# Cross-attention and FP4 FFN on one Trainium2 core: the hidden layer h quantized whole, one step behind its tile, and each engine's step written in a new order

## The chip, the cores and the metric

The kernel runs on one NeuronCore of one Trainium2 chip. The metric is the time on the device in microseconds (us), the median of several executions. The engines named below are TensorE (PE, matmuls), VectorE (DVE), ScalarE (ACT), GpSimd (POOL) and SyncE (SP, which here issues nearly all DMAs).

## What is computed

```python
x = x + attention(layernorm(x), ctx, mask)      # 16 heads of 32, 77 keys per batch
x = x + ffn(layernorm(x))                       # x is (4, 2048, 512)

def ffn(x):
    gate = fp4_linear(x, w_gate)                # 512 -> 1408
    y = fp4_linear(x, w_up)                     # 512 -> 1408
    h = silu(gate) * y
    return fp4_linear(h, w_down)                # 1408 -> 512

def fp4_linear(x, w):                           # both operands quantized in blocks of 16
    return fp4_quant_dequant(x) @ fp4_quant_dequant(w).T

def fp4_quant_dequant(x):                       # per block of 16 along the last axis
    scale = max(max(abs(block)) / 6, 1e-12)
    return round_to_grid(block / scale) * scale # grid 0, .5, 1, 1.5, 2, 3, 4, 6, with sign
```

The attention applies its projections Wq, Wk, Wv and Wo with biases, a softmax over the unmasked keys, and masks by batch 0's key lengths.

## The kernel before

**Tiles.** The 8192 rows of x are 64 tiles of 128 rows (16 tiles a batch). Every matmul operand is split into two bf16 halves, HI and LO, and a product is three matmuls (HI·HI, HI·LO, LO·HI; `split_product`, L537). The weights are quantized and transposed once, in the first 200 us; the last rows of the gate and up weights are woven into the first three steps (`weave`).

**A software pipeline.** One `step` works on six tiles at once, each in a different stage. In step s they are m = s+3 (first layernorm), n = s+2 (q, scores, softmax), a = s+1 (probabilities times v, output projection, residual, second layernorm, quantizing x), f = s (gate and up), d = s-1 (down projection) and e = s-2 (output). The same step is written out once for every engine; each engine runs its own list in order, and semaphores connect the lists. So a wait that is not met holds everything that stands behind it on that engine.

**TensorE (L604 to L689)** does in a step: probabilities times v of tile a (pv, 144 small matmuls), q of n, gate/up chunk 0 of f, mask and scores of n, output projection of a, gate/up chunk 1, the first 15 matmuls of the down projection of d (`down_part(0)`), gate/up chunks 2 and 3, and the last 18 matmuls of the down projection (`down_part(1)`). A gate/up chunk is 352 of the 1408 columns, 24 matmuls. Chunks 0, 1 and 3 share the PSUM banks 0 and 1; chunk 2 uses banks 2 and 3, which belong to the scores and to pv too. So chunk c+1 and the next pv wait until VectorE has read the earlier chunk (`h_done`).

**VectorE (L1091 to L1132)** multiplies silu(gate) by up (`h_chunk`, L1048), and quantizes h in two parts: columns 0 to 639 (part A) at the end of the step of tile f, once two chunks are there; columns 640 to 1407 (part B) in the following step. A part takes top (absolute maxima of the blocks, L875), scale (L881), inverse (L891), divide (L895), two rounding passes (L901, L905), rescale (L909) and the LO half (`half_low`, L863). Between divide and the first rounding ScalarE squares (L702); between rescale and the LO half ScalarE writes the HI half (L829, L853). The quantization of the 512 columns of x for tile a has the same chain.

**ScalarE** also applies silu (L771), the exponentials (L777), the HI halves of the probabilities (L784), and the application of both norms (L811, L832). Silu and exponential use different tables, so each step has two table loads. **GpSimd** computes the reciprocal root of both norms in three small instructions (L505, L507, L509) and adds the output bias to the residual's copy of x (L520).

**SyncE (L355 to L420)** issues one DMA after another and waits for each one's input in turn. The HI and LO halves reach TensorE through a transposing DMA (`transposed`, L353): of the attention output (oT), the normed x (xnT), the probabilities (pT, in two pairs), both parts of h (hT) and the quantized x (xqT). In the first step of a batch SyncE also issues the 12 loads of that batch's v (`load_values`, L306), right behind oT. hT has one buffer for each part, written again only after the down matmuls have read it.

**Probabilities.** The 77 keys are laid in 3 blocks of 32 (KJ = 3, KW = 96), so that a row group of 32 partitions holds one block; ScalarE and VectorE write all 96 columns of 8 heads, 768 elements a pair.

## Time and profile before

| what | before |
|---|---|
| median of 3 runs | 2188.06 us (2186.34 to 2188.51) |
| the profiled execution | 2190.24 us, its span 2188.5 us |
| PE busy | 1954.9 us, 89% of the span |
| DVE busy | 1884.1 us, 86% |
| ACT busy | 1191.9 us, 54% |
| POOL busy | 395.2 us, 18% |
| mean share of the DMA engines in use, 1200 to 1800 us | 54% |
| mean granted TensorE clock | 0.961 of 2.4 GHz |

The span runs from the first instruction to the last. Busy shares are means over three different stretches: the preparation of the weights (up to about 200 us, with PE at 12 to 20 us in 50), 59 steps of nearly equal length, and four shorter steps at the end in which the pipeline empties. The granted clock of TensorE is 1.00 in the steps and between 0.53 and 0.69 from 50 to 200 us. Among the page's groups of instructions, the matmuls of the down projection stand out on TensorE: 84.5 us of idle time right before them, 80.6 of which ended with a transposing DMA of h.

### The profile page before, as it was taken

The numbers are of one execution on the slowest core, as the hardware profiler recorded it, in microseconds if no ns is written. First come the engines' busy times: TensorE is split into PE (matmuls) and PEld (weight loads), VectorE is DVE, ScalarE is ACT, GpSimd is POOL, SyncE is SP. The second block draws the span as 40 slices with busy tenths as digits, with TensorE's granted clock in tenths as the row PEclk, the third lists the DMA queues.
The fourth block names the chain that finished last, engine by engine and source line by source line (L and its number), as shares of the span: only waits on it lengthen the run. The fifth ranks groups of instructions, "written<-read, shape, count | busy, mean of one in ns | idle before, by whom it ended". The sixth has DMA issues, their size and how long they took to land.

```text
span 2188.5 us, 63466 instructions
## 1 busy us (share of the span) xinstructions
PE 1954.9 (89%) x24768; PEld 1228.0 (56%) x24960; DVE 1884.1 (86%) x3188; ACT 1191.9 (54%) x2617; POOL 395.2 (18%) x523
## 2 busy tenths in 40 slices
PE   6334899999998999999998999999999999999987
PEld 4222556666565656665565566665655566665654
DVE  7767889898987898988987898989888898988975
ACT  4534556655664566555664566556654566556631
POOL 4543111111111111111111111111111111111100
PEclk9656999999999999999999999999999999999999
DMA  5322665555555555555545555555545555555543
GB/s 168 80 68 64 106 125 126 115 114 115 124 113 107 122 124 118 118 108 127 121 98 122 121 127 115 113 115 124 123 102 122 122 127 117 111 118 121 121 90 63
DMA packets 663013, 248.19 MB, mean 113 GB/s; under 512 B 614870, under 2 KB 615894, under 8 KB 662974
## 3 DMA queue, kind: packets, MB, share of 16 engines
q1 hardware_dynamic: 661390, 247.67, 51.3%
q8 instruction: 24, 0.39, 0.1%
q10 hardware_dynamic: 1584, 0.01, 0.0%
q14 instruction: 15, 0.12, 0.0%
HBM read 65.97 MB, written 34.82 MB: 46 GB/s over the span
## 4 chain that ended last, share of the span: by engine, by line
DVE 23%; PE 19%; issue 18%; DMA 12%; ACT 12%; POOL 9%; SPq 7%; another core or an unknown queue 1%; ACTq 0%; POOLq 0%; DVEq 0%
PE psum L539 13%; DMA ph_room<-h_room 11%; SPq L353 5%; DVE h_room L895 4%; PE psum L630 4%; DVE neg_max L1054 4%; ACT L771 3%; DVE p_h L863 3%; POOL ln_rstd L507 3%; ACT silu_g L771 2%; POOL ln_var_eps L505 2%; ACT io_room L811 2%; ACT p_h L784 2%; POOL h_room L480 2%; DVE ln_stats L1018 2%
## 5 line engine op out<-in xcount | busy, mean ns | idle before, releaser
L610 PE MATMUL psum<-wguT,t_room 128*128 128x352 bf16 x6144 | 947.9, 313 | 4.5 <-DVE h_room L1048 1.1
L610 PEld LDWEIGHTS psum<-wguT,t_room 128*128 128x128 bf16 x6144 | 598.3, 98 | 327.8 <-DVE h_room L1048 2.0
L539 PE MATMUL psum<-wdT,ph_room 128*128 128x512 bf16 x1985 | 469.3, 385 | 84.5 <-DMA ph_room<-h_room 80.6
L539 PEld LDWEIGHTS psum<-wdT,ph_room 128*128 128x128 bf16 x2112 | 203.8, 99 | 336.5 <-DMA ph_room<-h_room 103.4
L505 POOL TENSOR_TENSOR ln_var_eps<-ln_mean_var,eps 128x1 f32<-128x1 f32 x128 | 64.5, 504 | 1618.7 <-DVE ln_mean_var L1020 1077.0
L702 ACT ACTIVATE h_sq<-h_room 128x640 bf16<-128x640 f32 (+3 forms) x158 | 121.1, 767 | 247.1 <-DVE h_room L895 247.1
L777 ACT ACTIVATE probs<-psum,neg_max 128x77 f32<-128x77 f32 x1024 | 235.0, 350 | 11.2 <-DVE neg_max L1054 10.4
L539 PE MATMUL psum<-t_room,wqT 128*128 128x128 bf16 x3072 | 188.3, 222 | 2.3 <-issue 1.0
L771 ACT ACTIVATE silu_g<-psum 128x352 f32<-128x352 f32 x256 | 117.3, 458 | 119.9 <-PE psum L610 119.2
L539 PEld LDWEIGHTS psum<-t_room,wqT 128*128 128x128 bf16 x3072 | 178.2, 100 | 7.2 <-issue 1.4
L539 PE MATMUL psum<-woT,t_room 128*128 128x512 bf16 x704 | 165.8, 385 | 14.5 <-issue 9.7
L895 DVE SCALAR_TENSOR_TENSOR h_room<-h_room,h_sc 128x640 f32<-128x640 f32 (+1 forms) x128 | 150.9, 1179 | 4.4
L1048 DVE TENSOR_TENSOR h_room<-silu_g,psum 128x352 f32<-128x352 f32 x256 | 132.1, 516 | 17.1 <-ACT silu_g L771 9.5
L797 ACT CAST halves<-q_room 128x512 bf16<-128x512 f32 x64 | 39.6, 618 | 185.1 <-DVE q_room L1035 185.1
L863 DVE TENSOR_TENSOR h_room<-h_room 128x640 bf16<-128x640 f32 (+1 forms) x128 | 113.7, 889 | 28.0 <-ACT h_room L853 27.0
L853 ACT CAST h_room<-h_room 128x640 bf16<-128x640 f32 x64 | 46.4, 725 | 154.2 <-DVE h_room L909 154.2
L863 DVE TENSOR_TENSOR p_h<-probs,p_h 128x768 bf16<-128x768 f32 x128 | 123.6, 965 | 5.1 <-ACT p_h L784 2.2
L539 PEld LDWEIGHTS psum<-woT,t_room 128*128 128x128 bf16 x768 | 70.8, 99 | 86.6 <-issue 4.7
L905 DVE SCALAR_TENSOR_TENSOR h_room<-h_sq,h_room 128x640 f32<-128x640 bf16 (+1 forms) x128 | 113.5, 887 | 2.2
L909 DVE TENSOR_TENSOR h_room<-h_room,h_sc 128x640 f32<-128x640 f32 (+1 forms) x128 | 112.1, 876 | 2.3
L901 DVE SCALAR_TENSOR_TENSOR h_room<-h_sq,h_room 128x640 f32<-128x640 bf16 (+1 forms) x128 | 112.8, 881 | 1.0 <-ACT h_sq L702 0.9
L875 DVE TENSOR_REDUCE h_sc<-h_room 128x40 f32<-128x640 f32 (+1 forms) x128 | 112.8, 881 | 0.0
(100 smaller groups left out, 2471.5 us busy)
## 6 DMA issues: line engine op xcount, KB each, us to landing
io_room<-in_x_dram SPq DMA_DIRECT2D x128, 256.0 KB, 2.7
x_scratch<-x_new SPq DMA_DIRECT2D x64, 256.0 KB, 2.0
x_cur<-x_scratch SPq DMA_DIRECT2D x64, 256.0 KB, 3.4
out_dram<-io_room SPq DMA_DIRECT2D x64, 256.0 KB, 2.7
t_room<-halves SPq DMA_TRANSPOSE x192, 3.1
raw<-in_L_ffn_w_down_dram SPq DMA_DIRECT2D x4, 704.0 KB, 4.4
raw<-in_L_ffn_w_gate_dram SPq DMA_DIRECT2D x11, 256.0 KB, 2.7
raw<-in_L_ffn_w_up_dram SPq DMA_DIRECT2D x11, 256.0 KB, 3.0
```

What stands on the lines that cost most here:

```text
L539: ins = pe.matmul(dst, left(i), right(j), start=first and n == 0, stop=last and n == len(PRODUCTS) - 1)
L610: ins = pe.matmul(ps[:, 0:CW], xqT[:, i, kc, :], wguT[:, which, j, kc, cols], start=(kc == 0 and i == j), stop=(kc == KC - 1 and i == LO))
L702: act.activation(dst, val, ACT.Square, scale=GRID_SLOPE).then_inc(done, 1)
L771: act.activation(silu_g[:, c % 2, :], gate_ps[c][:, 0:CW], ACT.Silu).then_inc(silu_done, 1)
L777: ins = act.activation(probs[:, h, 0:KEYS], score_ps[:, r, g, :], ACT.Exp, bias=neg_max[:, h:h + 1])
L863: return own.did(dve.tensor_tensor(dst, ps, high, ALU.subtract), signal, value)
L875: step_of(job, dve.tensor_reduce(job.sc[:, 0, 0:job.nb], blocks(job.src), AX_X, ALU.max, apply_absolute_value=True))
L895: step_of(job, dve.scalar_tensor_tensor(blocks(job.val), blocks(job.src), TIES_DOWN, spread(job.sc, 2, job.nb), ALU.mult, ALU.mult), job.d ...
L901: step_of(job, dve.scalar_tensor_tensor(job.tot, job.sq, GRID_BASE, job.val, ALU.add, ALU.subtract))
L905: step_of(job, dve.scalar_tensor_tensor(job.tot, job.sq, GRID_BASE, job.tot, ALU.add, ALU.subtract))
L909: step_of(job, dve.tensor_tensor(blocks(job.res), blocks(job.tot), spread(job.sc, 1, job.nb), ALU.mult), job.done)
L1048: own.did(dve.tensor_tensor(h[:, c * CW:(c + 1) * CW], silu_g[:, c % 2, :], up_ps[c][:, 0:CW], ALU.mult), h_done, f * CHUNKS + (c + 1))
```

## The change

- h is quantized whole (1408 columns) in the step behind its tile, where it was two parts in two steps. The semaphores of the two parts become one set; each of the eight kinds of instruction runs once, on 1408 columns and 88 blocks; the two transposing DMAs of h become one.
- The down projection runs one step later: for tile e = s-2 instead of d, all 33 matmuls in one piece, behind the output projection and ahead of gate/up chunk 1. Chunks 1, 2 and 3 then follow one another. `tile_out` stays with tile e, and moves to a later place in the step.
- The 77 keys are laid in 3 blocks of 26 (KN = 26) inside the row groups of 32. ScalarE and VectorE write 3·26·8 = 624 elements a pair in place of 768; the columns that are left out are set to zero once at the start by GpSimd. Number and shape of the matmuls of pv stay.
- DVE, ACT and SP run their step in a new order; the two norms' statistics get other work between their two instructions. GpSimd's add to the residual copy (L520) now waits for the HI half of q as well (`qT_hi`).
- The weights' quantization uses a scale tile of its own (`w_sc`), with the same instructions.

The core of the diff:

```diff
@@ SyncE, step @@
+                def probabilities(pair):
...
                 weave("norm")
                 if a is not None:
                     after(o_lo, a + 1)
...
                 if values is not None:
                     after(pv_done, GH * n)
                     load_values(values)
+                if e is not None:
+                    after(out_ready, e)
+                    after(x1_stored, 16 * e + 16)
+                    sp.dma_start(x1_cur[:], one(x1_scratch, e)).then_inc(x1_loaded, 16)
+                weave("scores")
+                weave("first")
+                if keys is not None:
+                    after(s_ps, GH * n + GH)
+                    load_keys(keys)
+                if n is not None:
+                    probabilities(0)
                 if m is not None and existing(m + 1) is not None:
                     after(xn_ready, m + 1)
                     sp.dma_start(x_in, one(x_t, m + 1)).then_inc(x_loaded, 16)
+                if n is not None and existing(n + 1) is not None:
+                    after(mask_ready, n + 1)
...
+                    sp.dma_start(mask_raw[:], one(mask_t, j + 1 if keys is None else 0)).then_inc(mask_loaded, 16)
+                if n is not None:
...
+                    probabilities(1)
+                if m is not None:
+                    after(xn_lo, m + 1)
+                    after(q_ps, m)
+                    transposed(xnT.rearrange("p s k t -> p (s k) t"), xn_h.rearrange("p s d -> p (s d)"), xnT_loaded)
+                weave("end")
                 if e is not None:
                     after(out_ready, e + 1)
                     sp.dma_start(one(out_t, e), out_sb).then_inc(out_stored, 16)
                 if a is not None:
                     after(x1_done, a + 1)
                     sp.dma_start(one(x1_scratch, a), x1_new[:]).then_inc(x1_stored, 16)
                     if existing(a + 1) is not None:
                         sp.dma_start(xb, one(x_t, a + 1)).then_inc(xr_loaded, 16)
...
                     after(xq_lo, a + 1)
                     after(gu_ps, a * CHUNKS)
                     transposed(xqT.rearrange("p s k t -> p (s k) t"), xq_h.rearrange("p s d -> p (s d)"), xqT_loaded)
...
+                if d is not None:
+                    after(h_lo, d + 1)
+                    after(down_done, d)
+                    transposed(hT.rearrange("p s k t -> p (s k) t"), h_h.rearrange("p s w -> p (s w)"), hT_loaded)
@@ GpSimd, step @@
                     pool.wait_ge(xr_loaded, 16 * a + 16)
+                    if n is not None:
+                        pool.wait_ge(qT_hi, n + 1)
                     own.did(pool.tensor_tensor(xb, xb, bo_all[:], ALU.add), xb_ready, a + 1)
@@ TensorE, step, behind the output projection @@
+                weave("first")
+                if e is not None:
+                    pe.wait_ge(hT_loaded, 16 * e + 16)
+                    at_least(pe, out_ready, e)
+                    for k in range(IC):
+                        ins = split_product(down_ps, lambda s: hT[:, s, k, :], lambda s: wdT[:, s, k, :],
+                                            k == 0, k == IC - 1)
+                    ins.then_inc(down_done, 1)
                 if f is not None:
                     pe.wait_ge(h_done, f * CHUNKS + 1)
                     gate_up_chunk(1)
-                if d is not None:
-                    pe.wait_ge(hA_loaded, 16 * d + 16)
-                    at_least(pe, out_ready, d)
-                    down_part(0).then_inc(downA_done, 1)
-                weave("first")
-                if f is not None:
                     if n is not None:
                         pe.wait_ge(exp_done, 2 * n + 1)
                     gate_up_chunk(2)
                     pe.wait_ge(h_done, f * CHUNKS + 2)
                     gate_up_chunk(3)
-                if d is not None:
-                    pe.wait_ge(hB_loaded, 16 * d + 16)
-                    down_part(1).then_inc(down_done, 1)
@@ VectorE, step @@
                 run(a, normalised)
                 run(m, first_norm)
+                run(a, half_low, o_h, o_sb, o_hi, o_lo, a)
+                run(d, top, hj, (h_done, d * CHUNKS + CHUNKS) if d is not None else None)
+                run(m, first_norm_end)
                 weave("norm")
...
                 run(n, q_low)
+                run(d, scale, hj)
+                run(d, inverse, hj)
                 run(n, maximum, 0)
+                run(d, divide, hj)
                 run(n, maximum, 1)
                 weave("scores")
...
                 run(a, residual)
                 run(a, second_norm)
+                run(f, h_chunk, 0)
+                run(a, second_norm_end)
+                weave("first")
+                run(d, first_round, hj)
+                run(d, second_round, hj)
+                run(d, rescale, hj)
+                run(a, top, xj, (xn2_ready, a + 1) if a is not None else None)
+                run(a, scale, xj)
+                run(a, inverse, xj)
+                run(n, probabilities_low, 0)
                 run(m, half_low, xn_h, xn, xn_hi, xn_lo, m)
...
                 run(a, divide, xj)
+                run(n, probabilities_low, 1)
+                run(e, tile_out)
                 run(f, h_chunk, 1)
...
                 run(a, first_round, xj)
                 run(a, second_round, xj)
                 run(a, rescale, xj)
                 weave("end")
...
+                run(d, half_low, h_h, hq, h_hi, h_lo, d)
                 run(f, h_chunk, 2)
                 run(a, half_low, xq_h, xq, xq_hi, xq_lo, a)
...
                 run(f, h_chunk, 3)
```

The order of ScalarE's step after the change, tiles in brackets: HI half of the attention output (a); mask (n); q HI (n); silu 0 (f); exponentials of half 0 (n); square of h (d); first 4 exponentials of half 1; first norm and HI half of x (m); second norm `xn2` (a); HI half of probabilities pair 0; last 4 exponentials; HI half of h (d); HI half of pair 1; silu 1 (f); square of x (a); silu 2; HI half of the quantized x (a); silu 3.

## Rows read from the trace of the kernel before

**Rows 1.** VectorE groups, 1200-1800 us: instruction, count, busy us, mean ns, idle before.

```profile
L1048 DVE TENSOR_TENSOR h_room<-silu_g,psum 128x352 f32<-128x352 f32 x78 | 40.3, 516 | 2.6
L863 DVE TENSOR_TENSOR p_h<-probs,p_h 128x768 bf16<-128x768 f32 x40 | 38.2, 955 | 0.9
...
L895 DVE SCALAR_TENSOR_TENSOR h_room<-h_room,h_sc 128x768 f32<-128x768 f32 x20 | 31.4, 1572 | 0.7
L1054 DVE TENSOR_REDUCE neg_max<-psum 128x8 f32<-128x616 f32 x40 | 30.0, 793 | 0.0
...
L895 DVE SCALAR_TENSOR_TENSOR h_room<-h_room,h_sc 128x640 f32<-128x640 f32 x19 | 15.7, 825 | 0.7
...
L1068 DVE TENSOR_TENSOR x_new<-psum,io_room 128x512 f32<-128x512 f32 x20 | 13.7, 684 | 0.0
```

**Rows 2.** ScalarE groups, same view, same stretch.

```profile
L777 ACT ACTIVATE probs<-psum,neg_max 128x77 f32<-128x77 f32 x320 | 73.5, 351 | 0.2
...
L771 ACT ACTIVATE silu_g<-psum 128x352 f32<-128x352 f32 x78 | 35.8, 458 | 32.2 <-PE psum L610 32.0
L784 ACT CAST p_h<-probs 128x768 bf16<-128x768 f32 x40 | 33.1, 828 | 0.6
...
L777 ACT ACT_TABLE_LOAD x20 | 25.7, 1283 | 0.4
...
L829 ACT CAST h_room<-h_room 128x768 bf16<-128x768 f32 x20 | 16.9, 847 | 0.0
```

**Rows 3.** TensorE's down matmuls, same view, same stretch.

```profile
L539 PE MATMUL psum<-wdT,ph_room 128*128 128x512 bf16 x603 | 141.3, 382 | 22.5 <-DMA ph_room<-h_room 21.3 <-issue 0.2
```

**Rows 4.** TensorE timeline, one step: start us, length us, instructions, idle before.

```profile
1500.91 1.32 PE L630 MATMUL psum<-v_cur,ph_room 32*128 32x33 bf16 x144
...
1509.90 2.54 PE L539 MATMUL psum<-woT,t_room 128*128 128x512 bf16 x11 [0.16 <-issue]
...
1515.86 3.18 PE L539 MATMUL psum<-wdT,ph_room 128*128 128x512 bf16 x14
...
1531.41 1.32 PE L630 MATMUL psum<-v_cur,ph_room 32*128 32x33 bf16 x144
```

**Rows 5.** TensorE timeline: pv of step 3 and of step 62.

```profile
296.03 1.32 PE L630 MATMUL psum<-v_cur,ph_room 32*128 32x33 bf16 x144
...
2115.63 1.32 PE L630 MATMUL psum<-v_cur,ph_room 32*128 32x33 bf16 x144
```

**Rows 6.** Timeline of SyncE and TensorE, a batch's first step.

```profile
638.45 10.21 SPq L306 DMA_DIRECT2D v_cur<-v_scratch  x12
...
662.78 0.61 PE L539 MATMUL psum<-wdT,ph_room 128*128 128x512 bf16 x1 [5.42 <-DMA ph_room<-h_room]
```

**Rows 7.** Timeline of all engines: GpSimd's norm chain beside VectorE.

```profile
1504.29 0.19 POOL L505 TENSOR_TENSOR ln_var_eps<-ln_mean_var,eps 128x1 f32<-128x1 f32 x1 [17.52 <-DVE ln_mean_var L1020]
...
1514.79 0.93 DVE L909 TENSOR_TENSOR h_room<-h_room,h_sc 128x768 f32<-128x768 f32 x1
1514.95 0.81 POOL L505 TENSOR_TENSOR ln_var_eps<-ln_mean_var,eps 128x1 f32<-128x1 f32 x1 [7.87 <-DVE ln_mean_var L1074]
...
1515.63 0.69 DVE L863 TENSOR_TENSOR halves<-io_room,halves 128x512 bf16<-128x512 f32 x1
...
1515.84 0.88 POOL L507 TENSOR_TENSOR ln_rstd<-ln_var_eps,minus_half 128x1 f32<-128x1 f32 x1
...
1517.36 0.81 ACT L832 ACTIVATE q_room<-x_new,ln_shift,ln_rstd 128x512 f32<-128x512 f32 x1 [0.39 <-POOL ln_shift L509]
```

**Rows 8.** DMA issues, 1200-1800 us; last column median us to landing.

```profile
t_room<-halves SPq DMA_TRANSPOSE x59, 3.1
...
ph_room<-h_room SPq DMA_TRANSPOSE x38, 3.6
```

**Rows 9.** TensorE timeline, end of the program.

```profile
2156.82 7.32 PE L610 MATMUL psum<-wguT,t_room 128*128 128x352 bf16 x48
...
2178.26 6.73 PE L539 MATMUL psum<-wdT,ph_room 128*128 128x512 bf16 x17 [5.12 <-DMA ph_room<-h_room]
```

More of the change, by code:

```diff
@@ L90, in xattn_fp4_ffn_kernel @@
     h_fills = [range(c, min(c + 4, IC)) for c in range(0, IC, 4)]
-    H_KS = [range(0, 2 * CW // P), range(2 * CW // P, IC)]
-    H_PARTS = [slice(ks.start * P, ks.stop * P) for ks in H_KS]
     x_t = x.rearrange("b (t p) d -> (b t) p d", p=P)
@@ L152, in xattn_fp4_ffn_kernel @@
         hT_room = ph_room[:, 2 * GROUPS * KJ * P:]
-        hT = [hT_room[:, 2 * ks.start * P:2 * ks.stop * P].rearrange("p (s k t) -> p s k t", s=2, k=len(ks)) for ks in H_KS]
+        hT = hT_room.rearrange("p (s k t) -> p s k t", s=2, k=IC)
         x1_new = sb("x1_new", [P, D])
@@ L357, in step @@
                 n = existing(n)
+                def probabilities(pair):
+                    after(p_lo[pair], n + 1)
+                    after(pv_done, GH * n)
+                    transposed(pT[:, pair].rearrange("p s j g t -> p (s j g) t"),
+                               p_h[:, pair].rearrange("p s j w -> p (s j w)"), pT_loaded[pair])
                 weave("norm")
@@ L456, in _ @@
             own.did(pool.memset(probs[:], 0.0))
+            own.did(pool.memset(p_h[:].rearrange("p a s j w -> p (a s j w)").bitcast(U32), 0))
             own.after()
@@ L820, in step @@
                     exponentials(0, range(GROUPS))
+                weave("scores")
+                if d is not None:
+                    square(h_sq[:], hv, h_val, d + 1, h_square)
+                if n is not None:
                     act.wait_ge(s_max, 2 * n + 2)
                     exponentials(1, range(2)).then_inc(exp_done, 1)
-                    probabilities_high(0)
-                    exponentials(1, range(2, GROUPS)).then_inc(exp_done, 1)
-                weave("scores")
-                if d is not None:
-                    act.wait_ge(hB_ready, d + 1)
-                    at_least(act, hB_loaded, 16 * d)
-                    act.copy(h_h[1][:, HI], hq[:, H_PARTS[1]]).then_inc(hB_hi, 1)
+                if m is not None:
+                    act.wait_ge(ln1_rstd, m + 1)
+                    at_least(act, xn_lo, m)
+                    act.activation(xn, x_in, ACT.Identity, bias=ln1_shift, scale=ln1_rstd_sb)\
+                       .then_inc(xn_ready, 1)
+                    act.wait_ge(xn_ready, m + 1)
+                    at_least(act, xnT_loaded, 16 * m)
+                    act.copy(xn_h[:, HI], xn).then_inc(xn_hi, 1)
+                weave("first")
                 if a is not None:
@@ L833, in step @@
                        .then_inc(xn2_ready, 1)
+                if n is not None:
+                    probabilities_high(0)
+                    exponentials(1, range(2, GROUPS)).then_inc(exp_done, 1)
+                if d is not None:
+                    act.wait_ge(h_ready, d + 1)
+                    at_least(act, hT_loaded, 16 * d)
+                    act.copy(h_h[:, HI], hq).then_inc(h_hi, 1)
+                if n is not None:
+                    probabilities_high(1)
                 if f is not None:
                     silu_chunk(1)
-                if n is not None:
-                    probabilities_high(1)
-                weave("first")
                 if a is not None:
                     square(x_sq[:], xv, xq_val, a + 1, xq_square)
+                weave("end")
                 if f is not None:
                     silu_chunk(2)
-                weave("end")
                 if a is not None:
@@ L1080, in tile_out @@
                     own.did(dve.tensor_tensor(out_sb, down_ps, x1_cur[:], ALU.add), out_ready, e + 1)
-                def scales(job):
-                    scale(job)
-                    inverse(job)
                 def run(tile, operation, *args):
```

154 lines of the change are left out of this document (43 added, 111 removed).

## The prediction

> **What bounds the kernel now.** I read the shares of busy time first, then the timeline of one step on each engine, then who waited for whom. The page has TensorE at 89% and VectorE at 86%, with the preparation and the end in it; in a steady step both are nearly full. The step is the period from one pv to the next, 30.50 us [rows 4]; over the 59 steps from step 3 to step 62 the sum is 1819.6 us [rows 5], of which 59 × 30.50 = 1799.5 and 20.1 us extra. In the steady step TensorE has one real gap, ahead of the second part of the down projection: 21.3 us in 19 steps, 1.1 each [rows 3], ended by the transposing DMA of part B of h. Without it TensorE would need 29.4 us. The chain that ends last goes through that gap: exponentials, the LO half of the probabilities, the LO half of h's part B, SyncE's issue, 3.6 us to landing [rows 8], down matmuls, pv. So before is bound by a ring of VectorE, ScalarE and DMA that is 1.1 us longer than TensorE's own work.
>
> The extra 20.1 us are, but for 1 to 2 us of single late steps, the three first steps of a batch: SyncE spends 10.21 us on issuing 12 loads of v, everything behind them is late, and TensorE waits 5.42 us for h [rows 6].
>
> **The change, part by part.** Times t count from the start of pv; each engine's list is walked in its new order.
>
> *Instructions saved.* On VectorE 352, 512, 640 and 768 columns take 0.516, 0.684, 0.825 and 0.955 us, so about 1.04 ns a column and 0.15 us fixed [rows 1]; 1408 columns are 1.6 us where 640 + 768 were 1.78. Six wide kinds save about 0.18 each, scale and inverse about 0.15 each, and the divide of part B, 1.57 in place of the 0.95 that its width would take (GpSimd's residual add runs beside it), 0.6 more; two LO halves of probabilities go from 0.955 to 0.80. In all about 2.2 us of VectorE's step. On ScalarE 1408 columns are 1.45 us by the same slope (768: 0.847), a probability pair 0.71 for 0.828 [rows 2]. VectorE is not the bound by its work alone, then: about 25 of 29.4 us. What counts is the order.
>
> *Down projection.* Same 33 matmuls, at 15 in about 3.2 us [rows 4] 7.1 in one piece, now for a tile whose hT was issued early in the same step: its slack is over 4 us. The gap of 1.1 us goes. What is late next is the question.
>
> *First half of the step.* The output projection starts at 8.99 [rows 4], scores end just before. VectorE then runs maximum 0 (0.79), divide (1.6), maximum 1, residual, statistics (0.68 each), h_chunk 0 (0.52) and the short aggregate: from 9.0 to about 13.9, counting that an independent successor starts 0.08 us before its predecessor ends. Everything ahead (o, top, q LO, inverse) ends by 7.5 and has 1.4 us of cover.
>
> *GpSimd's norm chain.* This is where I choose. In before, L505 takes 0.81 us beside a rescale that runs until 1515.72, and ends with it at 1515.76; alone it takes 0.19. L507 starts at 1515.84 during a LO half that ends at 1516.32, and takes until 1516.72; the chain ends in xn2 at 1517.36, 2.4 us after its start [rows 7]. So each of the three waits out the VectorE instruction that reads two SBUF tensors. In the new order the chain starts at 13.95, in a first rounding pass of 1.6 us, then meets a second pass and a rescale of 1.6 each. If each holds it as in before, it ends at 13.9 + 4.8 + 0.15 = 18.9; if not, at 16.4.
>
> The Trainium skill says of this pair of ports (SBUF — State Buffer, section "SBUF: two separate sides") that it is an exclusive lock for a whole instruction, between a GpSimd operation and a VectorE operation with two SBUF inputs. By that rule wider VectorE instructions make every GpSimd operation beside them wait longer, which speaks against quantizing h whole; it would give the 18.9, without it 16.4. That the same waits occur in before agrees with it.
>
> *The rest of the ring.* ScalarE runs in order behind xn2: xn2 0.81, probabilities pair 0 0.71, four exponentials 0.9, HI half of h 1.45, pair 1 0.71, table load 1.28, silu 0.46 [rows 2, 7]. That is 6.3, less some 0.1 for each of four overlaps: silu 1 ends at 24.9. VectorE meanwhile does top, scale, inverse of x, LO of pair 0, LO of the normed x, divide of x, LO of pair 1 (ready at 23.1, ends at 23.9), output add. Then h_chunk 1 until 25.4 (TensorE wants it at 25.6 for chunk 3), three passes on x, 0.72 from start to start, until 27.6, LO half of h 1.6, h_chunk 2 until 29.5. The next pv needs h_chunk 2, for the banks of chunk 2 are its own. With 0.15 us for the semaphore pv starts at 29.65; without the overlaps on ScalarE at 29.95. I take **29.8 us a step**, bounds 29.4 (chain as short as in before, TensorE alone bounds) and 30.5. Gain: 59 × 0.7 = 41 us.
>
> *SyncE.* In the new order, nothing but a load stands between oT (issued about 4.4) and the first pair of probabilities (about 22). The 10.21 us of v loads fit in there, and I leave 2 of the 20.1 us: gain 18, bounds 12 and 20. The order behind is denser: pair 1 (LO ready 23.9) has 5.9 us to pv where before had about 9.8; a transposing DMA of this size took 3.6 to land [rows 8], so some 1 us of slack after queueing. The quantized x, ready at 30.1, has to land by 33.8; 3.1 us are needed. Then the whole h goes out (22 blocks of 128 columns against 10 or 12), and the next oT behind it. From the landings of 3.1 us for 8 blocks and 3.6 for 10 to 12, I estimate a start of 1.5 and 0.18 a block, 5.5 us for h. oT would land at about 8.7 for a start at 8.99: covered, barely.
>
> By the Trainium skill (DMA: Bandwidth & Descriptors, section "Latency and other measured facts") a transposing DMA may reach 261 GB/s. The 720 KB of h would then take 2.8 us to move, by an estimate from that page, and oT would have over 1 us of slack; by the landings above it has 0.3. The third case below would fall away by it.
>
> *Small parts.* GpSimd's new wait for q HI is met (about 5.4) before its norm chain lets it come to the add (about 7.2): nothing. What it prevents, the add beside the wide divide, would cost 0.6. Zeroing the probability room is one more instruction at the start, while every engine waits for the first weights: nothing, at most 1.5. Start, steps 0 to 2: no early down work and less quantizing, but chunk 3 waits for h_chunk 1 for 3 to 7 us with nothing to fill it: 0, bounds -5 and +4.
>
> *The end.* One step deeper, the pipeline empties more slowly. In before 24.4 us lie between the last gate/up matmul (at 2156.82 + 7.32 [rows 9]) and the end of the span. After, the last tile's h goes through one serial chain: silu and product 1.1, top, scale and inverse 2.6, divide 1.6, square 1.4, three passes 5.0, HI and LO 3.2 (14.9), transposing 6, then 33 matmuls. 17 of these took 6.73 us after a wait of 5.12 us [rows 9], against about 3.2 for 15 in a steady step [rows 4], so 33 take about 10; add and store 4. That is 35 in place of 24.4. The step before holds a whole down projection behind a late hT: 24 instead of 19. Step 62 saves 1. **End: +15**, bounds +8 and +20.
>
> *Sum.* -41 - 18 + 0 + 15 = -44 on the profiled span of 2188.5, so a span of 2144.5. The profiled execution was 2190.24, 2.2 over the median; the same difference on the median 2188.06 gives **2144 us**.
>
> **The rivals.**
> - *TensorE alone.* If GpSimd is not held by the long passes, or VectorE catches up, the step is 29.4: -65 - 18 + 15 = 2120. For it: VectorE's saved 2.2 us. Against it: rows 7.
> - *The DMA queue behind the whole h.* oT or the quantized x lands 0.3 to 0.6 us late in every step, since 22 blocks pass ahead of oT: step 30.1 to 30.4, in all 2162 to 2179. For it: slacks of 0.3 to 0.6 us, drawn from two landings. Against it: in before oT landed in time by the same 3.1 us.
> - *The ring closes as before.* Another wait takes the place of the removed one at 30.5, so the step does nothing and only SyncE's gain and the longer end are left: 2185.
> - *Slower: the second pair of probabilities.* Its transposing DMA stands behind a load of x, the mask's load and pair 0, and is issued 4 us nearer to pv than before. It decides from a landing 5.9 us after its LO half; break-even is 0.75 us past that. If queueing makes it 7.4, pv waits 1.4 us: step 31.2, 59 × 0.7 = +41, -3 for the rest, 2226. For it: about 1 us of slack is an estimate. Against it: a landing of 3.6 us leaves room for 2 us of queueing.
>
> **How the numbers follow.** Forecast 0.45, TensorE alone 0.25, queue behind h 0.15, ring as before 0.05, slower 0.10. The first three are all faster by more than 0.2% (4.4 us, about what a measurement of this kernel can tell from no change): 0.85; the ring as before is the same, 0.05; slower 0.10. The range takes the first three and the ring, with the start and the end at their bounds: 2108 to 2187. It leaves out the slower case and the tails.
>
> **What would show it.** A steady step of 29.8 with pv waiting 0.2 to 0.5 us for VectorE's product, and no wait of down matmuls; L505, L507 and L509 longer than 1 us each in the second chain; the divide of h at 1.6. First steps of a batch no longer than the others. Last gate/up matmul 35 us from the end. A step of 29.4, with GpSimd short, is the first rival; output projection or chunk 0 waiting for a DMA the second; pv waiting for a DMA the slower one. I would be wrong altogether if TensorE waited elsewhere by 1 us in each step.

## The result, and the profile after

| what | before | after |
|---|---|---|
| median | 2188.27 us (2186.34 to 2188.51) | 2170.74 us (2169.53 to 2174.64) |
| ratio | | 0.9925, 95% interval 0.9908 to 0.9942 |
| the profiled execution, its span | 2190.24, 2188.5 us | 2174.64, 2172.8 us |
| PE busy | 1954.9 us, 89% | 1977.6 us, 91% |
| DVE busy | 1884.1 us, 86% | 1763.1 us, 81% |
| POOL busy | 395.2 us, 18% | 523.7 us, 24% |
| pv of step 3, pv of step 62, end of the span | 296.03, 2115.63, 2188.5 | 290.56, 2079.76, 2172.8 |

The changed kernel is 17.5 us faster (0.75%), where 44 us were forecast. 2170.74 lies in the range and the sign is right, but less than half of the gain is there. The last line of the table splits the 15.7 us between the two spans: the start gives 5.5, the 59 steps give 30.4, the end takes 20.2 back. The rise of PE busy is no more work: both kernels run 24960 matmuls, and the trace of before lacks the records of 192 of them.

Groups of the page of after (columns as in [rows 1], the last being idle time before and its releaser) that answer to [rows 3] and [rows 7]; line numbers are a little lower than in before:

```profile
L607 PE MATMUL psum<-wguT,t_room 128*128 128x352 bf16 x6144 | 945.1, 314 | 48.1 <-DMA t_room<-halves 41.1
...
L536 PE MATMUL psum<-wdT,ph_room 128*128 128x512 bf16 x2112 | 469.0, 381 | 12.9 <-DMA ph_room<-h_room 12.9
L500 POOL TENSOR_TENSOR ln_var_eps<-ln_mean_var,eps 128x1 f32<-128x1 f32 x128 | 103.6, 809 | 1433.6 <-DVE ln_mean_var L1010 999.5
...
L536 PE MATMUL psum<-woT,t_room 128*128 128x512 bf16 x768 | 179.2, 384 | 11.8 <-DMA t_room<-halves 9.9
```

The wait of the down matmuls for h, 80.6 us in before, is 12.9, and all of it is at the end of the program (0.84 and 12.06). In its place the gate/up matmuls wait 41.1 us (6.9 of them at the end), and the output projection 9.9, for transposing DMAs of `halves` (quantized x and attention output); in [rows 4] the output projection has 0.16 us ahead of it, from no DMA.

The timeline of one steady step (start us, length us, instructions, idle before and releaser), cut to the issues of SyncE that matter and to what waits, answers to [rows 4] and [rows 7]:

```profile
1505.60 0.35 SPq L405 DMA_DIRECT2D x_scratch<-x_new  x1
1505.71 0.69 DVE L852 TENSOR_TENSOR halves<-q_room,halves 128x512 bf16<-128x512 f32 x1
1505.86 1.25 PEld L621 LDWEIGHTS psum<-v_cur,ph_room 32*128 32x128 bf16 x144 [0.29 <-DVE h_room L1040]
1505.87 1.35 PE L621 MATMUL psum<-v_cur,ph_room 32*128 32x33 bf16 x144
...
1506.13 0.35 SPq L407 DMA_DIRECT2D io_room<-in_x_dram  x1
...
1506.74 1.32 SPq L353 DMA_TRANSPOSE t_room<-halves  x1
...
1508.33 3.54 SPq L353 DMA_TRANSPOSE ph_room<-h_room  x1
...
1509.21 0.69 DVE L852 TENSOR_TENSOR halves<-q_room,halves 128x512 bf16<-128x512 f32 x1 [0.16 <-ACT halves L781]
...
1510.60 3.75 PE L607 MATMUL psum<-wguT,t_room 128*128 128x352 bf16 x24 [0.54 <-DMA t_room<-halves]
...
1512.47 1.24 SPq L353 DMA_TRANSPOSE t_room<-halves  x1
...
1515.55 0.80 DVE L1046 TENSOR_REDUCE neg_max<-psum 128x8 f32<-128x616 f32 x1 [2.17 <-PE psum L652]
...
1515.57 2.76 PE L536 MATMUL psum<-woT,t_room 128*128 128x512 bf16 x12 [0.15 <-DMA t_room<-halves]
...
1520.38 1.59 DVE L890 SCALAR_TENSOR_TENSOR h_room<-h_sq,h_room 128x1408 f32<-128x1408 bf16 x1
1520.55 1.48 POOL L500 TENSOR_TENSOR ln_var_eps<-ln_mean_var,eps 128x1 f32<-128x1 f32 x1 [6.53 <-DVE ln_mean_var L1069]
...
1522.01 1.62 DVE L894 SCALAR_TENSOR_TENSOR h_room<-h_sq,h_room 128x1408 f32<-128x1408 bf16 x1
1522.11 1.94 POOL L502 TENSOR_TENSOR ln_rstd<-ln_var_eps,minus_half 128x1 f32<-128x1 f32 x1
1523.67 1.62 DVE L898 TENSOR_TENSOR h_room<-h_room,h_sc 128x1408 f32<-128x1408 f32 x1
1524.14 1.28 POOL L504 TENSOR_SCALAR ln_shift<-ln_mean_var,ln_rstd 128x1 f32<-128x1 f32 x1
...
1525.46 0.81 ACT L819 ACTIVATE q_room<-x_new,ln_shift,ln_rstd 128x512 f32<-128x512 f32 x1 [3.69 <-POOL ln_shift L504]
...
1526.31 0.69 DVE L864 TENSOR_REDUCE x_sc<-q_room 128x32 f32<-128x512 f32 x1 [1.01 <-ACT q_room L819]
...
1536.13 1.35 PE L621 MATMUL psum<-v_cur,ph_room 32*128 32x33 bf16 x144
```

The step is 1536.13 - 1505.87 = 30.26 us (over 59 steps 1789.2, or 30.33 each; before 30.50 and 20.1 us extra). Read as a ring, it goes as follows. Chunk 0 of gate/up waits 0.54 us for the quantized x, issued 3.86 us earlier behind a store and a load of 256 KB each. The scores, the first maximum, and everything after it on VectorE are late by as much. GpSimd's three small instructions take 1.48, 1.94 and 1.28 us, and end 0.06, 0.42 and 0.13 us behind VectorE's three long passes. Then ScalarE applies the norm, VectorE quantizes x, and pv waits 0.29 for `h_chunk`. The LO half of the quantized x ends 0.53 us behind the start of pv (at 1506.40 in these rows), and its DMA is issued 0.34 later: again too late for chunk 0. The attention output (oT) has its own delay: its LO half ends at 1509.90, but SyncE is issuing the DMA of h from 1508.33 to 1511.87, and issues oT at 1512.47. The output projection starts 3.10 us after that.

The page of after shows the same ring: the chain that ended last lies 19% on TensorE, 18% on VectorE, 17% on GpSimd, 17% on SyncE's issuing and 11% on DMA.

### The profile page after: what moved, and what is told of

It is laid out like the page before. It is cut to its first block, busy times and chain, and to the rows that moved or that the text cites. A ratio compares the mean times of both kernels' runs of the same rounds, so it can differ in the third digit from the quotient of the medians.

```text
span 2172.8 us, 62951 instructions
## 1 busy us (share of the span) xinstructions
PE 1977.6 (91%) x24960; PEld 1233.6 (57%) x24960; DVE 1763.1 (81%) x2676; ACT 1150.7 (53%) x2489; POOL 523.7 (24%) x524
## 4 chain that ended last, share of the span: by engine, by line
PE 19%; DVE 18%; SPq 17%; POOL 17%; issue 12%; DMA 11%; ACT 5%; POOLq 0%; DVEq 0%; ACTq 0%; another core or an unknown queue 0%
PE psum L607 12%; SPq L353 11%; DMA t_room<-halves 11%; POOL ln_rstd L502 5%; POOL ln_var_eps L500 4%; DVE h_room L884 4%; POOL ln_shift L504 4%; DVE neg_max L1046 3%; PE psum L536 3%; POOL h_room L475 2%; DVE h_room L1040 2%; DVE x_new L1061 2%; ACT q_room L819 2%; PE psum L652 2%; DVE p_h L852 2%
## 5 line engine op out<-in xcount | busy, mean ns | idle before, releaser
L607 PE MATMUL psum<-wguT,t_room 128*128 128x352 bf16 x6144 | 945.1, 314 | 48.1 <-DMA t_room<-halves 41.1
L536 PE MATMUL psum<-wdT,ph_room 128*128 128x512 bf16 x2112 | 469.0, 381 | 12.9 <-DMA ph_room<-h_room 12.9
L500 POOL TENSOR_TENSOR ln_var_eps<-ln_mean_var,eps 128x1 f32<-128x1 f32 x128 | 103.6, 809 | 1433.6 <-DVE ln_mean_var L1010 999.5
L1046 DVE TENSOR_REDUCE neg_max<-psum 128x8 f32<-128x616 f32 x128 | 101.9, 798 | 145.6 <-PE psum L652 145.6
L819 ACT ACTIVATE q_room<-x_new,ln_shift,ln_rstd 128x512 f32<-128x512 f32 x64 | 52.0, 813 | 231.6 <-POOL ln_shift L504 231.6
L502 POOL TENSOR_TENSOR ln_rstd<-ln_var_eps,minus_half 128x1 f32<-128x1 f32 x128 | 155.5, 1215 | 10.0
L692 ACT ACTIVATE h_sq<-h_room 128x1408 bf16<-128x1408 f32 (+2 forms) x94 | 110.9, 1180 | 49.1 <-DVE h_room L884 49.1
L536 PEld LDWEIGHTS psum<-woT,t_room 128*128 128x128 bf16 x768 | 70.7, 99 | 96.8 <-DMA t_room<-halves 18.7
L852 DVE TENSOR_TENSOR p_h<-probs,p_h 128x624 bf16<-128x624 f32 x128 | 101.4, 792 | 12.0 <-ACT p_h L774 12.0
L592 PE MATMUL psum<-ident,h_room 128*128 128x128 f32 x88 | 24.1, 427 | 89.9 <-POOL h_room L479 89.9
L898 DVE TENSOR_TENSOR h_room<-h_room,h_sc 128x1408 f32<-128x1408 f32 x64 | 104.0, 1625 | 2.2
L894 DVE SCALAR_TENSOR_TENSOR h_room<-h_sq,h_room 128x1408 f32<-128x1408 bf16 x64 | 104.0, 1625 | 2.2
L852 DVE TENSOR_TENSOR h_room<-h_room 128x1408 bf16<-128x1408 f32 x64 | 103.6, 1618 | 0.8 <-ACT h_room L827 0.8
```

The costliest lines, as they stand in the source:

```text
L500: own.did(pool.tensor_tensor(var_eps, mean_var[:, 1:2], eps[:], ALU.add))
L502: own.did(pool.tensor_tensor(rstd, var_eps, minus_half[:], ALU.pow))
L536: ins = pe.matmul(dst, left(i), right(j), start=first and n == 0, stop=last and n == len(PRODUCTS) - 1)
L607: ins = pe.matmul(ps[:, 0:CW], xqT[:, i, kc, :], wguT[:, which, j, kc, cols], start=(kc == 0 and i == j), stop=(kc == KC - 1 and i == LO))
L692: act.activation(dst, val, ACT.Square, scale=GRID_SLOPE).then_inc(done, 1)
L852: return own.did(dve.tensor_tensor(dst, ps, high, ALU.subtract), signal, value)
```

## The experiments

The theories for the steady step: **Q**, SyncE's DMAs (what goes out ahead of the quantized x, and the whole h ahead of oT, makes them land late); **H**, the long passes hold GpSimd's chain, and the ring through it is longer than TensorE's work. Every ratio is against the kernel before in the same series. A line number in a fence is that of its own kernel.

**x_ahead.** SyncE issues the store of x1 and the load of the next residual x before the first pair of probabilities, not right ahead of the quantized x.

```diff
+                if a is not None:
+                    after(x1_done, a + 1)
+                    sp.dma_start(one(x1_scratch, a), x1_new[:]).then_inc(x1_stored, 16)
+                    if existing(a + 1) is not None:
+                        sp.dma_start(xb, one(x_t, a + 1)).then_inc(xr_loaded, 16)
                 if n is not None:
                     probabilities(0)
...
                 if a is not None:
-                    after(x1_done, a + 1)
-                    sp.dma_start(one(x1_scratch, a), x1_new[:]).then_inc(x1_stored, 16)
-                    if existing(a + 1) is not None:
-                        sp.dma_start(xb, one(x_t, a + 1)).then_inc(xr_loaded, 16)
                     after(xq_lo, a + 1)
```

> The changed kernel, with SyncE's store of x1 and load of the residual's x moved from right ahead of the quantized x's transposing DMA to ahead of the first pair of probabilities, where SyncE is idle. Theory Q (these 512 KB stand in the DMA queue ahead of the quantized x, which lands 3.8 us after issue instead of 3.1, and gate/up chunk 0 waits 0.54 us for it): the wait goes, step 29.7, about 30 us faster than the changed kernel, ratio to before about 0.978. Rival (VectorE's list alone sets the step, the wait of chunk 0 only fills what pv would wait otherwise): pv waits 0.5 us more for the product of chunk 2, step 30.2, ratio 0.992.

Measured: 2148.58 us, ratio 0.9813 (0.9797 to 0.983), 22 us less than after; step 29.9. Its timeline:

```profile
1516.32 1.24 SPq L353 DMA_TRANSPOSE t_room<-halves  x1
...
1519.80 3.75 PE L608 MATMUL psum<-wguT,t_room 128*128 128x352 bf16 x24
...
1525.17 2.54 PE L537 MATMUL psum<-woT,t_room 128*128 128x512 bf16 x11 [0.55 <-DMA t_room<-halves]
```

Chunk 0 starts 3.48 us after the issue, and waits for nothing. The DMA of the quantized x lands 3.2 to 3.4 us after its issue in ten steps of this run (1200 to 1500 us), and 3.5 to 4.0 in after; 0.1 us more comes from SyncE, which issues it 0.24 us behind the LO half and not 0.34. So the two transfers of 256 KB ahead of it were the 0.54 us. The gain is 22 us where 30 were expected, since now the output projection waits 0.55 us for oT. SyncE issues h's DMA ahead of it, which takes 3.44 us (1517.82 to 1521.26); the LO half of oT is ready at 1519.54, its issue comes at 1521.84, 2.30 us later.

**h_behind_o.** On top of x_ahead, SyncE issues h's DMA right behind the next oT, in the following step.

```diff
-                if d is not None:
-                    after(h_lo, d + 1)
-                    after(down_done, d)
-                    transposed(hT.rearrange("p s k t -> p (s k) t"), h_h.rearrange("p s w -> p (s w)"), hT_loaded)
...
+                if e is not None:
+                    after(h_lo, e + 1)
+                    after(down_done, e)
+                    transposed(hT.rearrange("p s k t -> p (s k) t"), h_h.rearrange("p s w -> p (s w)"), hT_loaded)
```

> x_ahead, with the transposing DMA of the whole h moved from the end of SyncE's step to behind the next oT. In x_ahead the output projection waits 0.55 us for oT. Theory W (the 22 blocks of h stand ahead of oT in the queue): that wait goes; h lands at about 11.0 for the down projection at 11.4, so no new wait, step 29.5 to 29.7 in place of 29.9, ratio to before 0.972 to 0.977. Rival (h now lands after 11.4): down waits what the output projection waited, step as in x_ahead or longer, 0.981 or more.

Measured: 2127.34 us, ratio 0.9718 (0.9702 to 0.9734), another 21 us less; step 29.50. The output projection no longer waits for oT, and no matmul waits for a DMA in a steady step:

```profile
1503.94 4.71 SPq L353 DMA_TRANSPOSE t_room<-halves  x2
...
1508.96 3.38 SPq L353 DMA_TRANSPOSE ph_room<-h_room  x1
...
1512.17 2.54 PE L537 MATMUL psum<-woT,t_room 128*128 128x512 bf16 x11 [0.16 <-issue]
```

The first line holds two issues, the quantized x and oT, the second from 1507.42, which is 0.24 us behind its LO half. So what held oT in after and x_ahead was not the landing, 3.1 us after its issue in after, but SyncE's own time for issuing h. The first steps of two batches are longer again (31.5 and 31.1 us), so the mean over the 59 steps is 29.65.

Both halves of Q are shown: removing both waits takes after from 30.3 to 29.5 us a steady step, 43 us in all, although GpSimd's chain keeps its length (1.48, 1.94 and 1.29 us here too).

**passes_split.** Each of the three passes over h in two instructions, 640 and 768 columns; SyncE's list is left as it is.

```diff
-                run(d, first_round, hj)
-                run(d, second_round, hj)
-                run(d, rescale, hj)
+                for operation in (first_round, second_round, rescale):
+                    for part in hparts:
+                        operation(part)
```

> The changed kernel, with each of the three passes over h behind the square (two roundings, rescale) as two instructions, 640 and 768 columns, the same work and six instructions in place of three; the norm's chain stays on GpSimd. Theory H: each of GpSimd's three instructions waits out a pass of 0.8 to 0.95 us instead of 1.6, the chain is 2.6 to 3.0 us instead of 5.0, VectorE doesn't lose time (independent neighbours overlap 0.08): step 29.4 to 29.6, ratio to before 0.972 to 0.975. Rival (GpSimd's instructions are slow for another reason than the width): the chain stays near 5 us, step 30.25 or a little longer, ratio 0.992 to 0.997.

Measured: 2127.64 us, ratio 0.9719 (0.9703 to 0.9735), 43 us less than after; step 29.5. In its timeline, one line holds the two VectorE instructions of a pass (x2):

```profile
1517.53 1.66 DVE L890 SCALAR_TENSOR_TENSOR h_room<-h_sq,h_room 128x640 f32<-128x640 bf16 x2
1517.69 0.68 POOL L500 TENSOR_TENSOR ln_var_eps<-ln_mean_var,eps 128x1 f32<-128x1 f32 x1 [5.85 <-DVE ln_mean_var L1076]
...
1518.44 1.15 POOL L502 TENSOR_TENSOR ln_rstd<-ln_var_eps,minus_half 128x1 f32<-128x1 f32 x1
1519.11 1.68 DVE L894 SCALAR_TENSOR_TENSOR h_room<-h_sq,h_room 128x640 f32<-128x640 bf16 x2
1519.69 1.15 POOL L504 TENSOR_SCALAR ln_shift<-ln_mean_var,ln_rstd 128x1 f32<-128x1 f32 x1
1520.71 1.69 DVE L898 TENSOR_TENSOR h_room<-h_room,h_sc 128x640 f32<-128x640 f32 x2
1520.88 0.81 ACT L819 ACTIVATE q_room<-x_new,ln_shift,ln_rstd 128x512 f32<-128x512 f32 x1 [1.91 <-POOL ln_shift L504]
```

GpSimd gets in between the halves: 0.68, 1.15 and 1.15, a chain of 3.2 us in place of 4.9. A pass is busy for 0.06 to 0.07 us more; from the first start to the last end the three take 4.87 us, whole they took 4.91. Chunk 0 no longer waits for its DMA in the steady step, with SyncE's list unchanged: x is quantized earlier in the step. So H is true as well. Q and H are not rivals: they are two sections of one ring. Taking 1.7 us out of the chain, or the two waits out of SyncE's section, is enough to bring the ring down to TensorE's own step, within 0.05 us. The chain run on VectorE in place of GpSimd was not measured.

**chain_alone.** VectorE waits for the norm before its first pass, so that GpSimd meets none.

```diff
+                if a is not None and d is not None:
+                    dve.wait_ge(ln2_rstd, a + 1)
                 run(d, first_round, hj)
```

> The changed kernel with one wait more: VectorE starts the first rounding pass over h only when GpSimd's norm chain is done, so the chain has nothing of VectorE beside it. Theory H: the chain takes about 1.3 us instead of 5.0 (0.2, 0.55, 0.27 and gaps). VectorE is idle 1.3 us there, but its waits further down (1.0 for xn2, 0.2 and 0.4 for ScalarE) go, so the step hardly moves: 30.0 to 30.3, ratio to before 0.988 to 0.993. Rival (the chain is slow by itself in this place): it stays at 4 us or more, and the step gets longer by the idle time, 32 to 34, ratio over 1.04.

Measured: 2181.47 us, ratio 0.9963 (0.9948 to 0.9977), 11 us more than after; the 59 steps are 30.51 each, for 30.33 in after.

```profile
1525.32 0.19 POOL L500 TENSOR_TENSOR ln_var_eps<-ln_mean_var,eps 128x1 f32<-128x1 f32 x1 [6.73 <-DVE ln_mean_var L1069]
1525.58 0.55 POOL L502 TENSOR_TENSOR ln_rstd<-ln_var_eps,minus_half 128x1 f32<-128x1 f32 x1
...
1526.23 0.26 POOL L504 TENSOR_SCALAR ln_shift<-ln_mean_var,ln_rstd 128x1 f32<-128x1 f32 x1
1526.53 1.63 DVE L890 SCALAR_TENSOR_TENSOR h_room<-h_sq,h_room 128x1408 f32<-128x1408 bf16 x1 [1.29 <-POOL ln_shift L504]
```

The chain alone is 1.2 us, which shows that the rest of the 4.9 is the long passes. The time missed the expectation: no step longer than in after was expected. The rows show why: x's top (the block maxima) stands behind the three passes on VectorE, and starts 20.9 us after pv here (1531.39 for a pv at 1510.47), 20.4 in after and 18.7 in passes_split. A short chain that is paid for with idle VectorE gives nothing.

**split_and_ahead.** passes_split and x_ahead together.

> passes_split and x_ahead together. In passes_split TensorE no longer waits in the steady step (29.5 us), so if its own work is the bound there, the second edit is worth nothing: ratio to before 0.971 to 0.973, step 29.5. If the DMA queue still holds something there, it gets faster by 5 to 15 us: 0.965 to 0.969.

Measured: 2119.04 us (2116.85 to 2122.02), ratio 0.9682 (0.9664 to 0.9701), faster than both kernels by 69 and 52 us. The second branch holds: but for the first and the last, the steps are all alike (29.44 to 29.55). The 59 are together 5.4 us shorter than in passes_split, and pv of step 3 comes 3.6 us earlier. 29.45 is TensorE's own step: the chain that ended last lies 87% on TensorE here. The 29.4 estimated for it in the prediction was right. Both repairs of 22 and 43 us together give 52, not 65, for the same reason.

**before_keys_26.** The kernel before, with keys in blocks of 26 and nothing else changed. The HI and LO halves of the probabilities are written as in the change, 26 of 32 columns of a block, over a room zeroed once (those lines are not shown below). **keys_32.** After, with blocks of 32.

```diff
@@ before_keys_26, on before @@
-    KW = KJ * DK
+    KN = -(-KEYS // KJ)
+    KW = KJ * KN
...
-                    keys = slice(j * DK, min((j + 1) * DK, KEYS))
+                    keys = slice(j * KN, min((j + 1) * KN, KEYS))
@@ keys_32, on after @@
-    KN = -(-KEYS // KJ)
+    KN = DK
```

> The kernel before, with the keys in blocks of 26 and nothing else. Its ring goes through the HI half of pair 1 on ScalarE, the LO half of pair 1 and then that of h's part B on VectorE: 0.1 and 0.15 us less, perhaps 0.15 more from pair 0. Step 30.1 to 30.3 instead of 30.5, ratio 0.989 to 0.994. If before is not bound there: 0.999 to 1.001.

> The changed kernel, with the 77 keys laid in blocks of 32 as before, so that the HI and LO halves of the probabilities cover 768 elements a pair again. In the ring of VectorE and ScalarE the HI halves of both pairs (0.12 each) and the LO halves (0.15 each) stand behind xn2. If the ring of GpSimd's chain, ScalarE and VectorE sets the step, it is 0.25 to 0.5 us longer: ratio to before 0.999 to 1.005, so the narrower keys would be worth all that the change gained. If the ring is elsewhere: no difference to the changed kernel, 0.992.

Measured: before_keys_26 2169.16 us, ratio 0.9904 (0.9882 to 0.9927), step 30.07; keys_32 2181.43 us, ratio 0.9962 (0.9951 to 0.9974), somewhat faster than expected. The narrow keys alone give 20 us in the kernel before, as much as the whole change. All the rest alone gives 7, and with the narrow keys it adds nothing (2170.74 against 2169.16). The first steps of a batch are still long in before_keys_26 (38.7, 39.3 and 35.0 us), and not in after. Over the start and the 59 steps, after is 13.8 us ahead of before_keys_26, although its normal step is longer (30.33 against 30.07); the end takes 19.9 us back.

**v_late.** After, with the 12 v loads issued right ahead of the second pair of probabilities and not behind oT. **before_v_spread.** Before, with them in four groups of three in different places of SyncE's step.

> The changed kernel, with the 12 loads of v moved from behind oT, where SyncE is idle for 16 us in the new order, to right ahead of the second pair of probabilities. Theory V (the long first steps of a batch in before are SyncE's 10.2 us of issuing that find no room ahead of the probabilities; the new order has that room): the three steps get 5 to 9 us longer, also by half clock behind the wait, in all 15 to 27 us slower than the changed kernel, ratio to before 0.999 to 1.005. Rival (before lost the time otherwise): no difference to the changed kernel, 0.992.

> The kernel before, with one edit: in the first step of a batch SyncE issues the 12 loads of v three at a time in four places of its step, not all in one piece behind oT. Theory V (before lost some 18 us in three such steps because SyncE was busy for 10.2 us in one piece): these steps come down from 34 to 37.8 us to 30.5 to 32, all else stays, 14 to 18 us faster than before, ratio 0.992 to 0.994. Rival (the loads themselves or the DMA engines cost it): no more than 4 us faster, ratio over 0.998.

Measured: v_late 2209.63 us, ratio 1.0101 (1.0081 to 1.012), 39 us more than after, where 15 to 27 were expected. The three first steps of a batch are 43.05, 43.49 and 41.68 us, 37 together over three normal ones:

```profile
648.37 11.72 SPq L306 DMA_DIRECT2D v_cur<-v_scratch  x12
661.71 1.48 SPq L353 DMA_TRANSPOSE ph_room<-p_h  x1
...
665.82 1.35 PE L621 MATMUL psum<-v_cur,ph_room 32*128 32x33 bf16 x144 [12.86 <-DMA ph_room<-p_h]
```

pv waits 12.86 us where it waits for nothing with the loads behind oT. That part of the forecast stands: the place of the loads in SyncE's order is worth what they take. before_v_spread missed: 2188.81 us, ratio 1.0002 (0.9993 to 1.0012). Cut into four groups the loads still cost as much (first steps of 37.0, 36.8 and 36.0 us, for 37.8, 37.6 and 34.1 in before). SyncE has no long idle piece in before: between oT and the pairs of probabilities the longest is 2.7 us in the step of [rows 4] (1511.50 to 1514.15). The timeline of before_v_spread:

```profile
653.32 2.90 SPq L308 DMA_DIRECT2D v_cur<-v_scratch  x3
...
657.86 1.46 SPq L355 DMA_TRANSPOSE ph_room<-p_h  x1
659.59 1.57 SPq L355 DMA_TRANSPOSE ph_room<-h_room  x1
...
663.53 0.61 PE L547 MATMUL psum<-wdT,ph_room 128*128 128x512 bf16 x1 [5.80 <-DMA ph_room<-h_room]
```

In after SyncE waits up to 13.9 us in one piece for the first pair of probabilities, and the loads end before it. It is the new order of everything else that makes this room, not the cutting.

**end_in_parts.** passes_split, with the last tile's h quantized, transposed and multiplied in two parts (640 and 768 columns).

> passes_split, and for the last tile alone h is quantized, transposed and multiplied in two parts (640 and 768 columns), with ScalarE's squares and HI halves of one part beside VectorE's work on the other. Theory E (the 20 us more at the end are the serial chain over the whole last h, 5.4 us of landing and 33 matmuls half of them at half clock): 6 to 10 us faster than passes_split, ratio to before 0.967 to 0.969. Rival (the end is bound by something else): as passes_split, 0.972.

Measured: 2125.64 us, ratio 0.971 (0.9693 to 0.9727): 2 us less than passes_split, a miss.

```profile
2103.71 0.82 DVE L885 TENSOR_TENSOR h_room<-h_room 128x640 bf16<-128x640 f32 x1
2104.68 0.96 DVE L885 TENSOR_TENSOR h_room<-h_room 128x768 bf16<-128x768 f32 x1 [0.16 <-ACT h_room L856]
2106.34 0.34 SPq L413 DMA_DIRECT2D out_dram<-io_room  x1
2106.86 3.03 SPq L364 DMA_TRANSPOSE ph_room<-h_room  x2
...
2110.61 9.79 PE L553 MATMUL psum<-wdT,ph_room 128*128 128x512 bf16 x32 [9.11 <-DMA ph_room<-h_room]
```

The first part's LO half stood behind the second part's passes and ended at 2104.53. Its DMA then stood behind the output store of the tile before (issued at 2106.34), so both DMAs went out together from 2106.86 and there was no early half. That a better order of the two parts gives the 6 to 10 us was not tried.

## Why the prediction was wrong, step by step

**What bounds the kernel before: right.** The gap ahead of the down projection is gone from the steady step, and TensorE's own step is 29.45 (29.4 forecast).

**GpSimd's chain: right.** Forecast 1.6 us an instruction and 5.0 in all, from [rows 7]; measured 4.9 (1520.55 to 1525.46). The chain took 1.2 us alone, 2.4 in before, 3.2 beside half passes and 4.9 beside whole ones. The trace agrees with the rule of an exclusive lock in the Trainium skill (SBUF — State Buffer, section "SBUF: two separate sides") in all four. VectorE's and ScalarE's part of the step was right too: from the first maximum to the last product before pv, 9.0 to 29.5 was forecast, and 9.68 to 30.18 measured, 20.5 both times. One term in it is off without effect: "the same slope" gives ScalarE 1.51 us for 1408 columns and not 1.45; measured were 1.37 and 1.43.

**The step that failed: the two DMAs that were "covered", in the paragraph on SyncE.** The first maximum comes 9.68 us after pv, 0.7 later than the walk had it, and the rest of the ring moves with it. The two DMAs of that paragraph were both given too little.

*The quantized x.* The walk had it ready at 30.1, 0.3 us into the next step, issued at once and landed 3.1 us later, the median of [rows 8], which left 0.6 us before chunk 0. Measured from pv at 1505.87, it is ready at 0.53, is issued at 0.87, and lands 3.7 us after that, behind a store and a load of 256 KB each; chunk 0 starts at 4.73, where the walk had 4.0.

*oT.* The walk had it "issued about 4.4" and asked only when it lands behind the 22 blocks of h. It is ready at 4.03, but issued at 6.60, because SyncE spends 3.54 us on issuing the DMA of h. The two parts of h in before took 1.29 and 1.59 us in the step of [rows 4]. The walk has no term for SyncE's own time on h; in h_behind_o, where h goes out behind oT, oT is issued 4.26 us after pv. From its issue to the output projection oT takes 3.10 us here, so its landing was not late. The DMA of h itself takes 5.3 us to land, for an estimate of 5.5. The view of [rows 8] for after:

```profile
t_room<-halves SPq DMA_TRANSPOSE x60, 3.5
ph_room<-p_h SPq DMA_TRANSPOSE x40, 3.8
ph_room<-h_room SPq DMA_TRANSPOSE x20, 5.3
```

So the second rival came: 30.1 to 30.4 us a step and 2162 to 2179 us were its numbers, 30.33 and 2170.74 are the measured ones. Its reason came only in part: 22 blocks hold oT by the time of their issue, and the quantized x is held by the two copies ahead of it. Its chance of 0.15 was too low. The "evidence against", that oT landed in time in before, was drawn from DMAs of 10 or 12 blocks. 59 steps at 30.33 in place of 29.8 are 31 us; the forecast had left 2 of them to the batches, and 29 us too much gain remain: this is the miss. The slower rival did not come: pv waits for no DMA in the steady step of after.

By the transfer rate in the Trainium skill (DMA: Bandwidth & Descriptors, section "Latency and other measured facts") the move of h takes 2.8 us, by the estimate in the prediction, and oT would not be late. No run here shows that rate by itself: of the 5.3 us to h's landing 3.5 are the issue, and it is the issue that makes oT late.

**First steps of a batch: right.** Forecast -18. The three were 17.9 us over 30.50 in before (37.78, 37.55 and 34.08), and in after none is longer than its neighbours.

**The start: just past its bounds.** 0 was forecast with -5 to +4, and -5.5 measured.

**The end: too low.** +15 forecast, +20.2 measured, just over the bound of 20. From the last gate/up matmul to the end, 35 was forecast and 33.5 measured (2139.33 to 2172.8). The missing term is before it: from pv of step 62 to there it is 59.6 us, 11.1 more than in before, where 4 were forecast. Timeline of TensorE, to set beside [rows 9]:

```profile
2084.55 6.42 PE L607 MATMUL psum<-wguT,t_room 128*128 128x352 bf16 x24 [3.47 <-DMA t_room<-halves]
...
2114.84 6.63 PE L607 MATMUL psum<-wguT,t_room 128*128 128x352 bf16 x24 [3.42 <-DMA t_room<-halves]
...
2159.52 10.04 PE L536 MATMUL psum<-wdT,ph_room 128*128 128x512 bf16 x33 [12.06 <-DMA ph_room<-h_room]
```

No tile is left whose q would stand between pv and chunk 0, and nothing covers the landing of the quantized x: 3.47 and 3.42 us of waiting, and both times 24 matmuls at a granted clock of 0.58 and 0.55 that take 6.4 and 6.6 us in place of 3.75. That is 12.4 us which the walk of the last steps did not contain; before had 4.2 us of waits in the same stretch (3.06 for oT, 1.11 for a product of VectorE). The 10 us for the last 33 matmuls was right (10.04).

**The sum.** Forecast -41 - 18 + 0 + 15 = -44; measured -30.4 for the steps and the batches, -5.5, +20.2, in all -15.7 on the span. Start and end are off by -5.5 and +5.2 and cancel; the 29 us of the steps are left. The profiled execution of after is 3.9 us over its median, before's was 2.0 over its own, 2188.27; hence -17.5 on the medians.

**The saving on the instructions** was taken as 2.2 us of VectorE with no effect of its own, since "VectorE is not the bound by its work alone". VectorE's busy time fell by 1.9 us a tile (121 us over 64). before_keys_26 shows that narrower probabilities, 0.25 to 0.4 us less in before's ring by its expectation, were worth 0.43 a step there. The prediction costed the change only whole; its best part needed none of the rest.

**The range.** Its upper end does not follow from its own rule: the ring as before, with -18 for the batches and the start and the end at +4 and +20, gives 2194 and not 2187. The measured time is not affected by it.

## What to carry to other kernels

In a ring that closes with a slack of tenths of a microsecond, a DMA's landing is not its median over all places. Look in its own place at two things: how long the issuing engine is still busy with the DMA ahead (3.5 us for the 22 blocks of h here), and which bytes go out just ahead of it. Move what is not urgent (stores, next loads, the large transfer) away from it. Where a short chain of GpSimd operations is on such a ring, keep the VectorE instructions with two SBUF inputs beside it short: cutting three of 1.6 us into two each cost VectorE no time from the first start to the last end, and gained 0.7 us a step. Price the parts of a bundled change one by one, since here one of them alone gave the whole gain.

## What was not expected of the hardware

- Cutting a pass of 1408 columns in two costs VectorE 0.06 to 0.07 us of busy time (1.59 to 1.66, 1.62 to 1.68, 1.62 to 1.69), less than the 0.15 us fixed for an instruction that [rows 1] gave: parts of 0.79 and 0.95 us take 1.66 together, so they overlap by 0.08.
- SyncE's issue of a transposing DMA grows with its blocks: 1.2 to 1.7 us for 8 to 12 of them, 3.4 to 3.9 for the 22 of h (after, 1200 to 1500 us). It is in after the larger part of the 5.3 us from the start of h's issue to its landing.
- Behind each wait of 3.4 us at the end, the granted clock over the next 6.5 us was 0.55 and 0.58, near the lower of TensorE's two levels (1.2 of 2.4 GHz); behind the 12 us wait it was 0.72 over the last 33 matmuls. In the steady steps it is 1.00.
- 12 loads of v are 10.21 us of SyncE's time in before, and 11.72 in both after and v_late, in two different places.
